# Attention of a fused layer: the small products of one sequence at four steps and in one bank, the score products for the exponentials in three banks

## What is computed

```python
h = _layernorm(x, ln1_g, ln1_b)
q, k, v = ((h @ W).reshape(B, 256, 16, 8) for W in (Wq, Wk, Wv))
scores = einsum('bqhd,bkhd->bhqk', q, k) / sqrt(8)
attn = softmax(scores, axis=-1)
x = x + einsum('bhqk,bkhd->bqhd', attn, v).reshape(B, 256, 128) @ Wo
m = _layernorm(x, ln2_g, ln2_b)
probs = softmax(m @ Wg)                     # 8 experts, the best 2 of each token
wts, idx = top_k(probs, 2)
x = x + sum over the two of wts * (gelu(m @ W1[e] + b1[e]) @ W2[e] + b2[e])
```

## Time and profile before

| | |
|---|---|
| three timed runs | 957.50, 957.54, 949.01 us; median 957.5 us |
| the profiled execution's own time | 945.66 us |
| its span, first to last instruction | 943.9 us |
| mean granted TensorE clock | 0.937 of full |
| attention stage | 206 to 645 us of the span |

### The profile page before, as it was taken

How to read it: one execution, slowest core, us unless ns; L and a number is a source line. 1 busy time by engine, 2 the same in 40 slices (tenths; PEclk the granted TensorE clock), 3 DMA queues, 4 the chain that set the end, 5 groups by cost and what they waited for, 6 DMA issues and landing times.

```text
span 943.9 us, 25402 instructions
## 1 busy us (share of the span) xinstructions
PE 755.6 (80%) x8206; PEld 456.1 (48%) x8206; DVE 801.8 (85%) x1727; ACT 633.0 (67%) x1270; POOL 522.8 (55%) x665
## 2 busy tenths in 40 slices
PE   3678776678999989898798989898889999999500
PEld 2444454423444534343343434345667888888400
DVE  7689989788898898989999898993888888888893
ACT  6655548837777778776668778676657778788400
POOL 9800169800226382631537887077857747777775
PEclk9989989968999999998989999899999999999955
DMA  8750005421122111220111222012445555655453
GB/s 209 256 209 1 1 4 186 154 85 41 48 58 58 49 51 48 58 58 19 35 36 55 72 69 64 2 31 63 107 107 135 136 116 142 147 143 145 114 162 97
DMA packets 130458, 84.23 MB, mean 89 GB/s; under 512 B 53398, under 2 KB 115994, under 8 KB 130346
## 3 DMA queue, kind: packets, MB, share of 16 engines
q1 hardware_dynamic: 122154, 65.93, 24.7%
q0 software_dynamic: 8192, 16.79, 7.0%
HBM read 30.77 MB, written 41.42 MB: 76 GB/s over the span
## 4 chain that ended last, share of the span: by engine, by line
PE 43%; POOL 19%; issue 12%; DVE 11%; ACT 8%; DMA 1%; DVEq 1%; ACTq 0%; POOLq 0%; SPq 0%
PE bank L1468 39%; POOL HT L769 7%; POOL Z L769 7%; ACT arena L868 5%; POOL xh L513 2%; PE bank L1663 2%; POOL rr L509 2%; DVE arena L1067 2%; DVE QK L1374 1%; DVE arena L1136 1%; PE bank L1472 1%; PE bank L1670 1%; ACT arena L777 1%; DVE QK L1371 1%; ACT arena L928 1%
## 5 line engine op out<-in xcount | busy, mean ns | idle before, releaser
L1136 DVE TENSOR_REDUCE arena<-bank 128x2 f32<-128x512 f32 x512 | 330.2, 685 | 41.1 <-PE bank L1468 37.2
L868 ACT ACTIVATE arena<-bank 128x512 f32<-128x512 f32 x512 | 288.9, 597 | 112.3 <-PE bank L1468 110.2
L1468 PE MATMUL bank<-QK 31*128 31x256 f16 (+1 forms) x2100 | 181.7, 283 | 46.6 <-ACT arena L868 23.8
L1468 PE MATMUL bank<-w2p,QK 128*128 x1248 | 201.2, 247 | 1.9 <-DVE arena L1388 1.9
L702 POOL DMA_INDIRECT expert_in<-HT,idx x128 | 130.2, 1017 | 65.9 <-issue 30.2
L1468 PE MATMUL bank<-wst,w1h 128*128 128x256 f16 x624 | 156.7, 274 | 11.4 <-DVE arena L1388 6.2
L928 ACT ACTIVATE arena<-bank,b1s 128x256 f32<-128x256 f32 x312 | 122.4, 475 | 49.7 <-PE bank L1468 44.0
L1468 PE MATMUL bank<-arena,VA 128*32 128x256 f32 x2048 | 142.7, 398 | 0.7 <-ACT arena L868 0.7
L1468 PEld LDWEIGHTS bank<-QK 31*128 31x128 f16 (+1 forms) x2100 | 53.8, 93 | 169.1 <-ACT arena L868 128.8
L1468 PEld LDWEIGHTS bank<-w2p,QK 128*128 128x128 f16 x1248 | 121.2, 98 | 13.0 <-issue 2.3
L1374 DVE TENSOR_TENSOR QK<-arena,QK 128x1024 f16<-128x1024 f32 x78 | 95.6, 1226 | 17.3 <-ACT QK L777 14.5
(11 more groups left out here) (172 smaller groups left out, 1146.5 us busy)
## 6 DMA issues: line engine op xcount, KB each, us to landing
QK<-qk_parts SPq DMA_DIRECT2D x96, 128.0 KB, 2.6
expert_in<-arena SPq DMA_DIRECT2D x39, 256.0 KB, 3.6
expert_out<-arena SPq DMA_DIRECT2D x78, 128.0 KB
qk_parts<-arena SPq DMA_DIRECT2D x16, 512.0 KB, 3.1
X<-x SPq DMA_DIRECT2D x8, 512.0 KB, 5.7
wst<-w SPq DMA_DIRECT2D x16, 256.0 KB, 2.8
out<-arena SPq DMA_DIRECT2D x16, 256.0 KB, 2.7
expert_in<-HT,idx POOLq DMA_INDIRECT x128
```

The costliest lines, as they stand in the source:

```text
L868: nc.scalar.activation(PT[t % 8], bank[3 + t % 2][:, :], ACT.Exp, scale=DH ** -0.5)\
L1136: V.tensor_reduce(nmax[n % 2][:, :, 4 * j + g], bank[u % 3][:, :].rearrange("p (q t) -> p q t", q=2), AX.X, ALU.max, negate=True).then_inc ...
L1468: return nc.tensor.matmul(dst, lhsT, rhs, start=start, stop=stop)
```

## The change

- `st_half` and `exp_step` rotate over banks 3, 4 and 7 (`ST`), and `st_waits` waits for the exponential of step t - 3.
- All small products go to bank 6. `max_t` writes its columns 256 to 511, the others columns 0 to 383 (`tp5_group` and `ctx_t` all 512).
- They stand at four steps: `tp5_group` at c = 0, now of the same block; `ctx_t` at c = 4; `ctx_n`, then `max_t` at c = 8; `ctx_o`, `b1_shift`, `counts` and `logits` at c = 12.
- A new `bank6_free` waits, ahead of `tp5_group` and `ctx_t`, for all readers of the bank in the block before.
- On ScalarE `mt_evac` moves from c = 0 to c = 2. On VectorE `ctx_norm` moves from c = 6 to 5, `read_logits` and `b1_add` to 13.
- The routing runs without the break: 65 steps from 16*r0+14.

```diff
+        ST = (3, 4, 7)
-                nc.scalar.activation(PT[t % 8], bank[3 + t % 2][:, :], ACT.Exp, scale=DH ** -0.5)\
+                nc.scalar.activation(PT[t % 8], bank[ST[t % 3]][:, :], ACT.Exp, scale=DH ** -0.5)\
...
-                    if c == 0 and group_at(b - 7) is not None:
+                    if c == 2 and group_at(b - 7) is not None:
                         mt_evac(group_at(b - 7))
...
-                        if 16 * r0 + 6 <= 16 * b + c < 16 * r0 + 22 or 16 * r0 + 37 <= 16 * b + c < 16 * r0 + 78:
+                        if 16 * r0 + 14 <= 16 * b + c < 16 * r0 + 79:
                             next(rest, None)
...
-                    if b > 0 and c == 6:
+                    if b > 0 and c == 5:
                         ctx_norm(b - 1)
+                    if c == 13 and group_at(b - 7) is not None:
+                        read_logits(group_at(b - 7))
+                    if c == 13 and 2 <= b < 2 + NE:
+                        b1_add(b - 2)
+                    if c == 13 and b - 1 in ROUTE:
+                        dve.wait_ge(cnt_sum, ROUTE.index(b - 1) + 1)
...
-                if t >= 2:
-                    pe.wait_ge(exp_done, t - 1)
+                if t >= 3:
+                    pe.wait_ge(exp_done, t - 2)
...
+            def bank6_free(b):
+                pe.wait_ge(nmt_ready, min(b + 1, NB))
+                used(pe, x3_ready, b - 1)
+                used(pe, lg_read, sum(group_at(n - 7) is not None for n in range(b)))
+                used(pe, b1_added, min(b - 2, NE))
+                used(pe, cnt_read, sum(r + 1 < b for r in ROUTE))
...
-                if c < 2 and 2 <= b < 2 + NE:
-                    b1_shift(b - 2, c)
-                if c in (3, 4) and group_at(b - 7) is not None:
...
+                if c == 0 and group_at(b - 7) is not None:
+                    bank6_free(b)
+                    tp5_group(group_at(b - 7))
+                if c == 4 and b > 0:
+                    bank6_free(b)
                     if group_at(b - 7) is not None:
                         pe.wait_ge(mt_ready, group_at(b - 7) + 1)
                     ctx_t(b - 1)
-                if b + 1 < NB and c == 8:
+                if c == 8:
+                    if b > 0:
+                        ctx_n(b - 1)
+                    if b + 1 < NB:
+                        max_t(b + 1)
+                if c == 12:
+                    if b > 0:
+                        ctx_o(b - 1, b + 1 < NB)
                     if 2 <= b < 2 + NE:
-                        pe.wait_ge(b1_added, b - 1)
+                        b1_shift(b - 2, 0)
+                        b1_shift(b - 2, 1)
+                    if b - 1 in ROUTE:
+                        counts(ROUTE.index(b - 1), bank[6][:, 352:352 + 2 * NE])
                     if group_at(b - 7) is not None:
...
+                        logits(group_at(b - 7), bank[6][:, 288:288 + 4 * NE], MT)
...
-                if b > 0 and c == 9:
-                    ctx_n(b - 1)
-                if b > 0 and c == 12:
-                    ctx_o(b - 1, b + 1 < NB)
-                if c == 13 and group_at(b - 6) is not None:
-                    tp5_group(group_at(b - 6))
```

More of the change, by code:

```diff
@@ L874, in max_evac @@
                     act.wait_ge(nmt_in[(n - 2) % 4], 16 * ((n - 2) // 4 + 1))
-                nc.scalar.activation(nmt[n % 2], bank[7][0:H, 0:SL], ACT.Copy, scale=1.0 / MUL)\
+                nc.scalar.activation(nmt[n % 2], bank[6][0:H, SL:2 * SL], ACT.Copy, scale=1.0 / MUL)\
                     .then_inc(nmt_ready, 1)
@@ L1143, in b1_add @@
                 V.tensor_tensor(b1s[:, FC * k:FC * k + FC], b1s[:, FC * k:FC * k + FC],
-                                bank[7][:, 256 + FC * k:256 + FC * k + FC], ALU.add).then_inc(b1_added, 1)
+                                bank[6][:, 320 + FC * k:320 + FC * k + FC], ALU.add).then_inc(b1_added, 1)
             def ctx_norm(b):
@@ L1158, in ctx_add @@
                 z2 = Z[:, 2 * b:2 * b + 2, :]
-                V.tensor_tensor(z2, bank[7][:, 0:2 * D].rearrange("p (n d) -> p n d", d=D), z2, ALU.add)\
+                V.tensor_tensor(z2, bank[6][:, 0:2 * D].rearrange("p (n d) -> p n d", d=D), z2, ALU.add)\
                     .then_inc(x3_ready, 1)
@@ L1174, in read_logits @@
                 g = k - GRP0[part]
-                V.tensor_copy(lgs[part][:, 4 * NE * g:4 * NE * g + 4 * NE], bank[7][:, 288:288 + 4 * NE])\
+                V.tensor_copy(lgs[part][:, 4 * NE * g:4 * NE * g + 4 * NE], bank[6][:, 288:288 + 4 * NE])\
                     .then_inc(lg_read, 1)
@@ L1195, in route @@
                 of_blocks = slice(TAB0[part], TAB0[part + 1])
-                sums = bank[1][:, 0:2 * NE] if part == NP - 1 else bank[7][:, 320:320 + 2 * NE]
+                sums = bank[1][:, 0:2 * NE] if part == NP - 1 else bank[6][:, 352:352 + 2 * NE]
                 def over_e(v):
@@ L1343, in _ @@
                         stat5(stats_at(b), c)
-                    if c == 5 and 2 <= b < 2 + NE:
-                        if group_at(b - 7) is not None:
-                            dve.wait_ge(lg_done, group_at(b - 7) + 1)
-                        b1_add(b - 2)
-                    if c == 6 and group_at(b - 7) is not None:
-                        read_logits(group_at(b - 7))
                     for r0, rest in zip(ROUTE, routes):
-                        if 16 * r0 + 6 <= 16 * b + c < 16 * r0 + 22 or 16 * r0 + 37 <= 16 * b + c < 16 * r0 + 78:
+                        if 16 * r0 + 14 <= 16 * b + c < 16 * r0 + 79:
                             next(rest, None)
@@ L1575, in st_half @@
                 k = QK[n % 4][32 * j:32 * j + 32, g, :, :]
-                return mm(bank[3 + t % 2][:, SL * kt:SL * kt + SL], k[:, 1, P * kt:P * kt + P], k[:, 0, :])
+                return mm(bank[ST[t % 3]][:, SL * kt:SL * kt + SL], k[:, 1, P * kt:P * kt + P], k[:, 0, :])
             def s_half(u, qt):
@@ L1641, in max_t @@
                     pe.wait_ge(nmt_ready, n)
-                    pe.wait_ge(x3_ready, max(n - 2, 0))
                 for qt in range(2):
-                    last = mm(bank[7][0:H, P * qt:P * qt + P], nmax[n % 2][:, qt, :], ident)
+                    last = mm(bank[6][0:H, SL + P * qt:SL + P * qt + P], nmax[n % 2][:, qt, :], ident)
                 last.then_inc(nmt_done, 1)
@@ L1649, in b1_shift @@
                     pe.wait_ge(wst_in[k % 2], 16 * (k // 2 + 1))
-                    pe.wait_ge(x3_ready, k + 1)
                 for c in range(FC // 2 * half, FC // 2 * half + FC // 2):
-                    last = mm(bank[7][:, 256 + FC * k + c:256 + FC * k + c + 1], wst[k % 2][:, P * c:P * c + P],
+                    last = mm(bank[6][:, 320 + FC * k + c:320 + FC * k + c + 1], wst[k % 2][:, P * c:P * c + P],
                               aff[:, 3:4])
@@ L1677, in ctx_o @@
                 for qt in range(2):
-                    last = mm(bank[7][:, P * qt:P * qt + P], CNT[:, P * qt:P * qt + P], wos[:, :])
+                    last = mm(bank[6][:, P * qt:P * qt + P], CNT[:, P * qt:P * qt + P], wos[:, :])
                 last.then_inc(wo_done, 1)
+            def bank6_free(b):
[4 more added lines that the diff above has]
+                used(pe, cnt_read, sum(r + 1 < b for r in ROUTE))
             def tp5_group(k):
@@ L1774, in _ @@
                     pv((t - 6) // 4)
-                if c < 2 and 2 <= b < 2 + NE:
-                    b1_shift(b - 2, c)
-                if c in (3, 4) and group_at(b - 7) is not None:
-                    pe.wait_ge(x3_ready, b - 1)
-                    pe.wait_ge(lg_read, group_at(b - 7))
-                    logits(group_at(b - 7), bank[7][:, 288:288 + 4 * NE], MT, range(2 * c - 6, 2 * c - 4))
-                for part in range(NP - 1):
-                    if c == 3 and b == ROUTE[part] + 2:
-                        pe.wait_ge(x3_ready, b - 1)
-                        counts(part, bank[7][:, 320:320 + 2 * NE])
-                if b > 0 and c == 5:
+                if c == 0 and group_at(b - 7) is not None:
[3 more added lines that the diff above has]
+                    bank6_free(b)
                     if group_at(b - 7) is not None:
@@ L1807, in _ @@
                     experts(-3)
-                if b == NB and c == 10:
+                if b == NB and c == 9:
                     experts(-2)
```

6 lines of the change are left out of this document (1 added, 5 removed).

## The result

The changed kernel takes 963.9 us (median of four, 960.1 to 973.7) against 953.7 us (also of four) for the kernel before beside it. The ratio of the executions is 1.0144, 95% interval 1.0093 to 1.0195; the two medians alone give 1.011. It is slower by 1 to 2 percent, where 17 us less were forecast. The profiled execution took 966.18 us against 945.66; its span is 964.4 us. The loss is in attention: the last exponential ends at 666.3 us in place of 645.2, and what follows is as long as before.

What follows compares the result with a forecast made beforehand. It took attention to be bound by VectorE and TensorE waiting in turns, neither full. Ordinary blocks -6.5 and -4.5, routing -2.5 and end -3.5 gave -17 us, from 957.5 to 940.5 us, range 921 to 966.

Steps and rivals of the forecast that it cites:

- the price of the moved `b1_shift`: Blocks with `b1_shift` at c = 12: 12.45 us as the group, 13.4 with both products, VectorE starved 1.5.
- The walk through the block: Start-to-start prices followed through one attention block: a plain block 11.85 us for 12.77, four ordinary blocks 49.05 for 51.2.
- The wait at c = 4: TensorE waits about 1.2 us ahead of `ctx_t` for ScalarE's copy; VectorE idles 0.95 us before maximum 5.
- The pairs: Score steps between small products and `pv` run two in a row, 0.33 us for 2 x 0.32: up to eight times 0.3 a block.
- The third bank: Score steps wait for exponential t - 3, so exponentials never hold a step again and waits like the 0.67 us vanish.
- what is late next: Once exponentials no longer hold score steps, the other ring does: a step waits for the maximum of u - 3.
- Routing and end: Routing in one piece covers the c = 4 wait, -2.5 us; the last four blocks save -3.5, the softest number.
- up to 6 us: Width for TensorE's clock falling to 1.2 GHz, about 2 us a fall where VectorE isn't full; none expected in ordinary blocks.
- C: Rival, chance 0.15: `ctx_n` at c = 8 waits for a late `ctx_norm`, 0.9 to 1.0 us a block, 970 us.
- three signs of being wrong: Wait at `ctx_t` under 0.5 us, `ctx_n` at c = 8 waiting over 0.7, or experts' stage not starting as much earlier.
- B: Rival, chance 0.27: hand-overs eat the gain, 0.55 us more a block, by `mt_evac` behind exponential 2 and c = 8 waiting 0.5; 957.
- A: Rival, chance 0.15: the c = 4 wait hides, VectorE becomes full in attention, only its work is left: -35 us, 922.

Runs made afterwards that it cites:

- e1: Changed kernel with GpSimd's norm of the router input ahead of the weight split that waits for `b1_shift`: 956.0 us, ratio 1.005 to the kernel before.
- e8: Kernel before with `b1_shift` moved to c = 12 and `b1_add` to c = 13: 966.8 us, ratio 1.0115 to the kernel before.
- e3: Changed kernel with the third bank taken away, exponentials' products on banks 3 and 4: 969.2 us, ratio 1.0187 to the kernel before.
- e9: Changed kernel with GpSimd's norm ahead of the weight split, ScalarE's context copy ahead of exponential 3, and two banks: 940.4 us, ratio 0.9869 to the kernel before.
- e2: Changed kernel with ScalarE's copy of the context ahead of exponential 3: 945.8 us, ratio 0.9933 to the kernel before.
- e11: Kernel before with ScalarE's copy of the context ahead of exponential 3: 955.9 us, ratio 1.0011 to the kernel before.
- e7: Kernel before with its routing in one piece, steps 20 to 78 behind 16*r0: 960.6 us, ratio 1.0115 to the kernel before.
- e5: Changed kernel with a pause in its routing, steps 14 to 31 and 48 to 80 behind 16*r0: 970.2 us, ratio 1.0178 to the kernel before.
- e6: Changed kernel with useless filler products into bank 6 in the routing blocks: 975.7 us, ratio 1.0204 to the kernel before.

## Why the prediction was wrong

**The step that failed first is the price of the moved `b1_shift`** ("With `b1_shift` as group (12.45), with both 13.4 (VectorE starved 1.5)"). It gave `b1_shift` at c = 12 a price on TensorE and on VectorE (13.4 us for a block with both products) and none on GpSimd. Its reader there, `split_weight`, waits for it, and `normed5` is queued behind. The prediction named `bank6_free` and what it asks of VectorE and held the wait at 0 to 0.3 us, but never asked where `xh5` comes from, though `tp5_group` had already waited 0.37 us for it in block 6 of the kernel before. Measured: 8.0 us of waiting in block 7 and 5.5 us of slower blocks around it in the profile, 9 us by the ratios (e1), and about 11 us when the same move is made in the kernel before (e8). Without this stall the kernel is still slower than before, by 0.5 percent (e1), so the rest of the forecast gain has to be looked for in the walk and in the routing.

**The walk through the block had the right mechanism and too small a size.** The wait at c = 4 was there in every block (1.25 to 1.45 us outside the routing, 0.5 to 1.4 in it), ahead of `ctx_t`, with ScalarE's copy as releaser, and VectorE idle ahead of maximum 5: 1.36 and 1.03 us for 1.2 and 0.95 in a plain block. `mt_evac` added nothing to it in group blocks, as said. The pairs came, step 9 and 10 went singly, `ctx_n` waited 0.19 for 0.2. But a plain block took 12.2 and not 11.85 us, a group block 12.8 to 13.0 and not 12.45, one with `bn_stats` 12.8 to 13.0 and not 12.3. (Its reading of the earlier trace rows has a slip that changes nothing: TensorE's second wait of 0.67 us, at 511.38, is ahead of step 5, not step 4.)

Three terms were too small. First, I had a reader start 0.05 us behind the end of what it waits for, as a score step does after an exponential; between copy and transpose it is 0.25 (528.85 to 529.10). That isn't a matter of the two engines: `ctx_n`, the same kind of transpose, started 0.06 us behind VectorE's norm, and `ctx_o` 0.05 behind ScalarE's copy. Behind the end of the copy the trace has two wait instructions of TensorE, L1657 (the copy's) at 528.9 and L1659 at 529.0, and then the transpose at 529.1. So the waits and their order may be what costs; no run moved them.

Second, idle of VectorE was booked too low: 0.60 and not 0.5 at c = 12 of a group block, and behind two `pv` of a plain one 0.14 us. Such a break costs more than it shows, 0.22 (526.98 to 527.80 for 0.60), because a maximum that follows another starts before that one's 0.68 us are over.

Third, a block with `bn_stats` was put at 12.3, below what VectorE's work comes to by the prediction's own terms, 10.75 + 1.6 = 12.35. In the kernel before it took 12.4 us (blocks 21 and 25) and VectorE never stood still over 0.12 us, so it had nothing to gain. In the changed kernel VectorE's wait at c = 4 is largely covered there, as said, but the 0.29 and 0.39 us that are left come on top.

For blocks 21 to 24 the forecast was -2.15 us: -0.9 in the plain block, -1.2 in the two group blocks, -0.1 in the one with `bn_stats`. Measured were -0.6, -0.3 and +0.4. Each miss is a few tenths; the forecast gain, 0.54 us a block, was itself the difference of such terms. Seven ordinary blocks (21 to 27) gained 0.7 us in all where 3.8 were due.

**The third bank** was said to end all waits for exponentials. They nearly ended, 2.9 us in attention for 23.4, but 14 of these 20.5 us came with the placing alone, and it gave about nothing: by e3 4 us, by e9 none in the ratios and 3 us in the medians, all within what the intervals leave open. The waits of the earlier trace rows were real, but the maxima stood right behind them, as the prediction's own "what is late next" says, and took over what the bank freed (e3); it then still booked the gain of the pairs to the block. What does help is the hand-over: the copy one instruction earlier gives 20 us (e2), and only in this placing (e11).

**Routing and end, -2.5 and -3.5 us, were +2.7 and +5.1** in the profiled executions. The routing covered the wait at c = 4 only in part: 0.5 to 1.4 us of it are left in blocks 17 to 20. The VectorE work was counted rightly (48.3 us in the last four blocks for 49.6), the clock was not: "up to 6 us" and "no fall" outside the routing. Attention spent 82 us at half clock in place of 27, of which the stall of block 7 (61 without it, e1) and the chance of the two executions can be a part. The 2 us that the prediction gives as the cost of a fall are worked out from no row and no run shows them; in e7 a single fall lasted 41 us and its two blocks took 16.6 us longer. e7 shows the loss by the one-piece routing alone, 11 us in the kernel before, which lie in the last four blocks, with TensorE full at 0.52 to 0.57 of the clock. That the same part of the changed kernel's +5.1 us is the clock is likely, by its 0.82 for 0.91, and not shown; e5 and e6 both failed to get it back.

**The rivals.** It came out as C said by size, slower by over 1%, but not by C's mechanism: the wait at c = 8 was 0.19 us (0.38 with `bn_stats`), not 1 us more. Of the prediction's three signs of being wrong, the two at c = 4 and c = 8 stayed quiet, since neither looks at GpSimd; the third came, the experts' stage starts 21 us later in the profiled execution. B comes nearest for the ordinary blocks, where the hand-overs ate most of the gain, though not by the two terms that B names. A, and with it the rule of the Trainium skill (Trainium Kernel Development and Optimization, Performance Expectations) as I had read it for this case, didn't come: in attention (from 222 us) weight loads were busy 176 of 444 us, 40%, and matmuls 366, 82%. TensorE had room on both counts, and the kernel got slower by waiting in order. That is no contradiction to the page, which speaks of the distance to a roofline.

**The sum by parts**, in the profiled executions, whose difference is some 7 to 10 us larger than that of the timed ones; attention's end is 21.1 us later: blocks 6 to 9 +15.5; the end +5.1; blocks 16 to 20 +2.7; blocks 1 to 5 +0.9; 21 to 27 -0.7; 10 to 15 nothing; block 0 and the start -2.2, with rounding.

## What to carry to other kernels

When a product is moved to a later step, follow every semaphore that it raises into the other engines' programs, and read what is queued behind the waiting instruction there; here the costly one was an engine that nobody looked at, since it was only 55 percent busy. Before giving a ring another buffer, look what ends next to it: a buffer is worth at most the distance to the second-latest wait, while an earlier place for the one instruction that a hand-over waits for (a copy ahead of, not behind, an unrelated one) gave 20 us. A gain of 4% of a block made of ten terms of 0.1 us should be forecast as no change until one of those terms has been seen in its new place.

## What the runs showed of the hardware

- In e7 a stretch at VectorE's pace was paid for twice. TensorE was busy 11.83 of its 16.0 us, at full clock; from 620 us on TensorE ran at 1.2 GHz for 41 us, though it was busy in 40.77 of them. First a row of e7, then one of the changed kernel's last block, at 2.4 GHz:

```profile
620.00:661.00 41.00, 40.77 (x272) 18.79 (x268) 19.10 (x49) 18.48 (x34) 22.87 (x23) 0.50 0.14 40
```

```profile
653.00:666.40 13.40, 12.29 (x150) 7.16 (x150) 2.56 (x10) 10.20 (x21) 10.26 (x11) 1.00 0.24 69
```

That is 150 matmul records in 13.4 us at full clock against 272 in 41 us at half.

- Of the clock between 222 us and the end of attention, the mean granted share was 0.97 before and 0.91 in the changed kernel, though its TensorE work is the same. These are one execution each; over whole executions the clock was 0.916 to 0.937 before and 0.902 to 0.916 in the changed kernel.
- From the end of an exponential to the score product that waited for it pass 0.05 us in the kernel before. From VectorE's norm to the fp32 transpose `ctx_n` it is 0.06, from ScalarE's copy to the products `ctx_o` 0.05. From ScalarE's copy to the fp32 transpose `ctx_t`, with two wait instructions of TensorE in between, it is 0.25 (median of 31).
- Two maxima in a row start 0.60 us apart though each takes 0.68 us. After an idle of 0.14 us the next one starts 0.82 us behind the last.
